# Turning the normalised rows by VectorE block transposes and a DRAM trip in a one-core language-model tower

## The reference

```
h  = weight[x] * keep_mask[x]                        # gather of rows, 32 x 512 x 256
n1 = layernorm(h)
u, res = split(n1 @ in_proj_w.T, [512, 256])
u  = causal depthwise conv of 4 taps along the tokens (u) + conv_b
delta = softplus(u @ dt_proj_w.T + dt_proj_b)        # 512 x 512
g  = u * sigmoid(delta)
y[t] = 0.9 * y[t-1] + 0.1 * g[t]                     # scan along the tokens
h  = h + y @ out_proj_w.T + res
n2 = layernorm(h)
xd = mx_quantise(n2)                                 # blocks of 32, fp6 grid, scaled back
h  = h + xd @ mx_quantise(ffn_weight).T + ffn_bias
```

## Time and profile before

| what | value |
|---|---|
| median of 3 runs | 1011.38 us (1007.56 to 1011.82) |
| profiled execution, its own time | 1011.74 us |
| its span from first to last instruction | 1009.9 us |
| PE busy | 970.3 us (96%) |
| PEld busy | 822.0 us (81%) |
| DVE busy | 854.6 us (85%) |
| ACT busy | 582.3 us (58%) |
| POOL busy | 743.1 us (74%) |
| chain that ended last | PE 93%, DVE 4%, POOL 1%, ACT 1%, DMA 1%, issue 1% |

### The profile page before, as it was taken

One profiled execution on the slowest core, in us unless ns is written; L12 is line 12 of the kernel. 1 busy time (PEld: TensorE's weight loads), 2 busy tenths in 40 slices (PEclk: granted clock), 3 DMA queues, 4 the chain that ended last, 5 costly groups with the idle time before them and its releaser, 6 DMA issues.

```text
span 1009.9 us, 15142 instructions
## 1 busy us (share of the span) xinstructions
PE 970.3 (96%) x5140; PEld 822.0 (81%) x5140; DVE 854.6 (85%) x1563; ACT 582.3 (58%) x966; POOL 743.1 (74%) x586
## 2 busy tenths in 40 slices
PE   3699999999999999999999999999999999999996
PEld 2477888888888888888888888888888888888885
DVE  4868988888988898888888898889888888889866
ACT  4455665565566565566556556656556655655441
POOL 5657777788777788777778877778877777886661
PEclk9799999999999999999999999999999999999997
DMA  4002122222211222211222221122221122221111
GB/s 152 22 21 63 55 56 80 83 64 85 76 55 56 83 62 83 83 55 54 78 83 62 83 77 55 55 83 62 83 83 53 56 78 83 63 84 64 42 43 42
DMA packets 51468, 68.28 MB, mean 68 GB/s; under 512 B 10096, under 2 KB 42736, under 8 KB 51440
## 3 DMA queue, kind: packets, MB, share of 16 engines
q1 hardware_dynamic: 45296, 51.08, 16.0%
q0 software_dynamic: 6144, 16.85, 6.4%
HBM read 35.40 MB, written 32.51 MB: 67 GB/s over the span
## 4 chain that ended last, share of the span: by engine, by line
PE 93%; DVE 4%; POOL 1%; ACT 1%; DMA 1%; issue 1%; DVEq 0%; POOLq 0%
PE psZ L991 12%; PE psZ L992 12%; PE psZ L998 12%; PE psT L949 6%; PE psT L945 6%; PE psT L946 6%; PE psU L934 6%; PE psU L930 6%; PE psU L931 6%; PE psO L1035 3%; PE psO L980 3%; PE psO L981 3%; PE psO L1036 3%; PE psO L982 3%; PE psO L1037 3%; PE psT L1049 3%
## 5 line engine op out<-in xcount | busy, mean ns | idle before, releaser
L356 POOL TENSOR_TENSOR g_lo<-g,g_hi 128x512 fp32r<-128x512 f32 x128 | 194.5, 1530 | 168.1 <-ACT g_hi L484 168.1
L683 DVE SCALAR_TENSOR_TENSOR u<-psU,cw,u 128x511 f32<-128x511 f32 x378 | 265.0, 743 | 18.6 <-ACT u L466 14.2
L991 PE MATMUL psZ<-u_hi,dt_hi 128*128 128x512 f32 x512 | 206.6, 404 | 10.3 <-ACT u_hi L473 7.1
L998 PE MATMUL psZ<-u_lo,dt_hi 128*128 128x512 f32 x512 | 204.1, 399 | 0.1
L992 PE MATMUL psZ<-u_hi,dt_lo 128*128 128x512 f32 x512 | 203.8, 398 | 0.0
L363 POOL TENSOR_TENSOR u_lo<-u,u_hi 128x512 fp32r<-128x512 f32 x128 | 163.3, 1299 | 15.3 <-ACT u_hi L473 14.0
L466 ACT ACTIVATE u<-psU,cb,cw 128x512 f32<-128x512 f32 x126 | 98.1, 779 | 121.8 <-PE psU L934 115.0
L477 ACT ACTIVATE psZ<-psZ,gate_b 128x512 f32<-128x512 f32 x128 | 84.5, 661 | 113.7 <-PE psZ L998 113.0
L341 POOL DMA_INDIRECT rows<-table,ids x128 | 126.3, 986 | 30.7 <-issue 29.4
L473 ACT ACTIVATE u_hi<-u 128x512 fp32r<-128x512 f32 x128 | 80.5, 629 | 91.9 <-DVE u L683 91.9
L767 DVE SCALAR_TENSOR_TENSOR g<-psZ,u 128x512 f32<-128x512 f32 x128 | 85.4, 687 | 45.6 <-ACT psZ L477 45.6
(11 more groups left out here) (107 smaller groups left out, 2186.7 us busy)
## 6 DMA issues: line engine op xcount, KB each, us to landing
out<-h SPq DMA_DIRECT2D x31, 512.0 KB, 2.9
turned<-xb SPq DMA_DIRECT2D x30, 512.0 KB, 2.8
xT<-turned SPq DMA_DIRECT2D x120, 128.0 KB, 3.5
rows<-table,ids POOLq DMA_INDIRECT x128, 2.9
dt_stage<-dt_wT SPq DMA_DIRECT2D x1, 1024.0 KB, 5.6
g<-in_wT SPq DMA_DIRECT2D x1, 768.0 KB, 4.6
ids<-x SPq DMA_DIRECT2D x32, 2.0 KB, 3.7
ow_stage<-out_wT SPq DMA_DIRECT2D x1, 512.0 KB, 7.4
```

What stands on the lines that cost most here:

```text
L356: pool.tensor_tensor(g_lo[:, m, :], g[:, m, :], f32(g_hi[:, m, :]), ALU.subtract).then_inc(g_lo_ready[m], 1)
L683: dve.scalar_tensor_tensor(u[:, m, back:T], u_psum_tile(st, m)[:, 0:T - back], cw[:, m, TAPS - 1 - back:TAPS - back], u[:, m, back:T], ALU ...
L991: pe.matmul(psZ[:, m % 2, :], dt_hi[:, k, o], u_hi[:, k, :], start=(k == 0), stop=False)
L998: ins = pe.matmul(psZ[:, m % 2, :], dt_hi[:, k, o], u_lo[:, k, :], start=False, stop=(k == M - 1))
```

## The change

The eight PE transposes of `n1` in each step go (the lead-in keeps its own), and `n1` is turned as `xd` is: `normalise1` writes it in the order of blocks, DVE transposes its 32x32 blocks into `nb_blocks` (`turn_n1`), SP writes those to `turned_n` in DRAM, waits, and reads them back in four DMAs into `nT` in SBUF. `nT_hi` and `nT_lo` are then made from `nT` on the same two engines as before. With this come changes of order: on DVE `turn_blocks` goes ahead of the convolution, gate 3 goes into the next step behind it, the taps of groups 0 and 1 alternate, `add_linear` goes ahead of `split_nT`, and gate 2 goes behind the quantisation; on ACT the first tap of group 1 goes ahead of `g_hi` 3, and `xT_hi` ahead of `u_hi` 3. The last step's `inverse_root2` on POOL is done in one part.

```diff
+        nb_blocks, nT = sb("nb_blocks", [P, C * D]), sb("nT", [P, C * D])
+        turned_n = nc.dram_tensor("turned_n", (P, C * D), F32, kind="Internal").ap()
...
+        n1_blocks = n1[:].rearrange("p c d -> p (c d)").rearrange("p (q k c j) -> p k q c j", q=Q, k=KD, c=C)
+        nT_by_token = nT[:].rearrange("p (a m i) -> p m a i", a=Q, i=BLOCK)
...
+                if st.front:
+                    sp.wait_ge(nT_lo_ready, s + 1)
+                    sp.wait_ge(n_turned, s + 1)
+                    sp.dma_start(turned_n, nb_blocks[:]).then_inc(n_written, 16)
+                    sp.wait_ge(n_written, 16 * (s + 1))
+                    for q in range(Q):
+                        blocks = turned_n.rearrange("(a j) (q n) -> q j a n", a=Q, q=Q)[q]
+                        sp.dma_start(nT[q * BLOCK:(q + 1) * BLOCK, :].rearrange("j (a n) -> j a n", a=Q),
+                                     blocks).then_inc(nT_loaded, 16)
...
-                    if later(s + 1):
-                        act.wait_ge(t1_psum, s + 1)
+                    if st.first:
+                        act.wait_ge(t1_psum, 1)
+                    elif st is not lead_in:
+                        act.wait_ge(n_turned, s)
...
 def split_nT():    # ACT
-                    act.wait_ge(t1_psum, s + 2)
+                    act.wait_ge(nT_loaded, Q * 16 * (s + 1))
...
-                    act.activation(nT_hi[:, nb], psT[:], ACT.Copy).then_inc(nT_hi_ready, 1)
+                    act.activation(by_token(nT_hi[:, nb]), nT_by_token, ACT.Copy).then_inc(nT_hi_ready, 1)
...
+                def turn_n1():
+                    dve.wait_ge(n1_ready, s + 2)
+                    if later(s):
+                        dve.wait_ge(n_written, 16 * s)
+                    dve.transpose(nb_blocks[:], flat(n1[:])).then_inc(n_turned, 1)
...
 def split_nT():    # DVE
+                    if st is not lead_in:
+                        dve.tensor_tensor(by_token(nT_lo[:, nb]), nT_by_token, f32(by_token(nT_hi[:, nb])),
+                                          ALU.subtract).then_inc(nT_lo_ready, 1)
+                        return
...
                 if st.tail:
                     dequantise(None, own=False)
-                convolve(0, 0, 1, 0, 1, 1)
-                if st.tail:
                     turn_blocks()
+                if st.back:
+                    gate(M - 1, s - 1)
+                convolve(0, 1, 0, 1, 0, 1)
+                if st.front:
+                    turn_n1()
...
+                if st.tail:
+                    add_linear(None)
                 if st.front:
                     split_nT()
-                if st.tail:
-                    add_linear(None)
                 if st.back:
                     block_max(None)
-                gate(2)
-                if st.back:
                     quantise()
                     dve.wait_ge(q_ready, s)
-                gate(3)
+                gate(2)
...
-                if st.front:
-                    transpose_n1()    # PE, between merge(1) and dt_proj_0_1((2, 3))
```

More of the change, by code:

```diff
@@ L192, in lm_tower_kernel @@
         turned_written, xT_loaded = sem("turned_written"), sem("xT_loaded")
+        n_turned, n_written, nT_loaded = (sem(n) for n in ("n_turned", "n_written", "nT_loaded"))
         xT_hi_ready, xT_lo_ready = sem("xT_hi_ready"), sem("xT_lo_ready")
@@ L376, in inverse_root2 @@
                     pool.wait_ge(var2_ready, s + (part or 0))
+                    if later(s - 1):
+                        pool.wait_ge(n2_ready, s - 1)
                     pool.tensor_tensor(rstd2[:, cs], ve2[:, cs], neg_half[:, cs],
@@ L390, in split_xT @@
                     pool.wait_ge(xT_hi_ready, s - 1)
-                    pool.tensor_tensor(by_token(xT_lo), xT_by_token, f32(by_token(xT_hi)),
+                    pool.tensor_tensor(by_token(xT_lo[:]), xT_by_token, f32(by_token(xT_hi[:])),
                                        ALU.subtract).then_inc(xT_lo_ready, 1)
@@ L425, in step @@
                 if st.back:
-                    for part in st.back_parts:
-                        inverse_root2(part)
+                    inverse_root2(None)
                 if st.main:
@@ L500, in normalise1 @@
                     act.wait_ge(nmr1_ready, s + 2)
-                    if later(s + 1):
-                        act.wait_ge(t1_psum, s + 1)
+                    if st.first:
+                        act.wait_ge(t1_psum, 1)
+                    elif st is not lead_in:
+                        act.wait_ge(n_turned, s)
                     for c in range(C):
-                        ins = act.activation(n1[:, c, :], h[:, ring, c, :], ACT.Identity, bias=nmr1[:, c:c + 1],
+                        to, h_c = n1[:, c, :], h[:, ring, c, :]
+                        if st is not lead_in:
+                            to, h_c = n1_blocks[:, :, :, c, :], h_c.rearrange("p (k q j) -> p k q j", k=KD, q=Q)
+                        ins = act.activation(to, h_c, ACT.Identity, bias=nmr1[:, c:c + 1],
                                              scale=rstd1[:, c:c + 1])
@@ L529, in split_xT @@
                         act.wait_ge(xT_loaded, Q * 16 * (s - 1))
-                        act.activation(by_token(xT_hi), xT_by_token, ACT.Copy).then_inc(xT_hi_ready, 1)
+                        act.activation(by_token(xT_hi[:]), xT_by_token, ACT.Copy).then_inc(xT_hi_ready, 1)
                         return
@@ L538, in split_nT @@
                 def split_nT():
-                    act.wait_ge(t1_psum, s + 2)
+                    if st is lead_in:
+                        act.wait_ge(t1_psum, 1)
+                        act.activation(nT_hi[:, nb], psT[:], ACT.Copy).then_inc(nT_hi_ready, 1)
+                        return
+                    act.wait_ge(nT_loaded, Q * 16 * (s + 1))
                     if later(s):
                         act.wait_ge(m_psum[1], s)
-                    act.activation(nT_hi[:, nb], psT[:], ACT.Copy).then_inc(nT_hi_ready, 1)
+                    act.activation(by_token(nT_hi[:, nb]), nT_by_token, ACT.Copy).then_inc(nT_hi_ready, 1)
                 if st is lead_in:
@@ L761, in add_linear, with gate @@
                                       ALU.add).then_inc(result_ready, 1)
-                def gate(m):
+                def gate(m, s=s):
                     dve.wait_ge(tanh_ready[m], s + 1)
@@ L837, in turn_blocks @@
                     dve.transpose(xb[:], flat(xd[:])).then_inc(xb_ready, 1)
+                def turn_n1():
[3 more added lines that the diff above has]
+                    dve.transpose(nb_blocks[:], flat(n1[:])).then_inc(n_turned, 1)
                 def split_nT():
                     dve.wait_ge(nT_hi_ready, s + 2)
-                    if later(s):
-                        dve.wait_ge(m_psum[1], s)
+                    if st is not lead_in:
+                        dve.tensor_tensor(by_token(nT_lo[:, nb]), nT_by_token, f32(by_token(nT_hi[:, nb])),
+                                          ALU.subtract).then_inc(nT_lo_ready, 1)
+                        return
                     dve.tensor_tensor(nT_lo[:, nb], psT[:], f32(nT_hi[:, nb]), ALU.subtract).then_inc(nT_lo_ready, 1)
@@ L1059, in transpose_n1 @@
                 def transpose_n1():
[L1060 to L1066, removed]
                     to_channels(lambda c, k: n1[:, c, k * P:(k + 1) * P], psT, t1_psum)
```

6 lines of the change are left out of this document (3 added, 3 removed).

## The result

The changed kernel takes 1021.62 us (median of 4 runs, 1019.36 to 1022.44), the kernel before, beside it, 1011.49. The ratio is 1.0106, with a 95% interval of 1.0076 to 1.0136: 10 us or 1% slower. The forecast was 1024 (994 to 1032), slower. The profiled execution's own time is 1021.15 us, its span 1019.3.

A forecast was written before the change was run, and what follows sets the result against it. PE bounds the kernel before at 29.83 us a step; afterwards a DVE, ACT and POOL loop of 30.30 us binds. 1011.74 + 13.6 - 0.9 = 1024.4, 0.36 less against the median: 1024 us, range 994 to 1032.

The forecast's parts named there:

- The layout: One middle step's DVE, ACT and POOL loop, counted from the variance instruction: 30.30 us against 29.83 before; chance 57%.
- POOL's stretch: POOL's run without a gap from g_lo 3 to the end of xT_lo, 15.96 us, ending at 30.36.
- this last term: Lead-in and steps 0, 1 and 31, without the loop: between 0 and -1.7 us, taken as -0.9.
- the wrong term: Trip of n1 through DRAM costs nothing; lead-in and first steps change by between 0 and -1.7 us each at most.
- The total of 1.3 us a step: PE's waiting in each middle step, about 1.3 us, most of it at linear for xT_lo.
- Two conflicts: DVE waits for POOL twice a step: nT_lo 0.97 us behind g_lo 0, the -mean instruction about 1.1 behind xT_lo.
- This mis-sized term: DVE reaches the small -mean instruction at 29.2 at the latest and waits about 1.1 us for xT_lo.
- Rival 2: nT_lo starts before g_lo 0, so POOL waits: loop 29.33 us, total 996.3 us; chance 15%.
- Its counterargument: With a shorter loop, add_linear and POOL's part both hang on the same xT_lo, restoring g_lo 0 first.
- Rival 3: DVE waits for POOL at nT_lo but not at the -mean instruction: loop 30.12 us, total 1019.2 us; chance 7%.
- Rival 1: Neither nT_lo nor the -mean instruction waits for POOL, PE stays the bound: 985.6 us; chance 9%.
- Rival 4: nT_lo waits for both g_lo, 1.27 us a step more, 1061; or late trip or lower PE clock; chance 9%.

The follow-up runs named there:

- e4: The changed kernel without the trip of n1 through DRAM, nT_hi and nT_lo reading nb_blocks directly; 1018.08 us.
- e6: The changed kernel with split_nT ahead of add_linear and the two small variance instructions moved from DVE to ACT; 985.02 us.
- e2: The changed kernel with nT_lo reading the PSUM tile psT in place of nT in SBUF, order unchanged; 995.6 us.
- e1: The changed kernel with split_nT put back ahead of add_linear on DVE, nothing else different; 996.66 us.
- e9: The changed kernel with DVE's old order around the gates, but split_nT still behind add_linear; 1013.9 us.
- e3: The changed kernel with DVE transposing only 32 of the 1024 columns of n1 (except in step 0); 1020.88 us.
- e5: The changed kernel with -mean and variance+eps of the second layernorm made on ACT in place of DVE; 1013.5 us.
- e7: The changed kernel with DVE's old order around the gates, split_nT ahead of add_linear; ACT's order as changed; 987.1 us.

## Why the prediction was right

**What bounds.** As forecast, PE's 0.87 us a step were given, and a loop of DVE, ACT and POOL took the bound over. The layout against the trace, counted from `ve` at 499.03:

| point | laid out | measured |
|---|---|---|
| gate 0 | 2.23 | 2.13 |
| `nT_lo` starts | 4.56 | 4.48 |
| `g_lo` 0 starts | 4.26 | 4.27 |
| block maxima start | 6.66 | 6.57 |
| gate 3 starts | 12.98 | 12.87 |
| POOL's stretch begins | 14.40 | 14.26 |
| `xT_lo` ends | 30.36 | 30.22 |
| next `ve` | 30.30 | 30.16 |

Every point held within 0.15 us. Against its own execution the forecast of 1024.4 was 3.3 us too high: 29 steps of 30.30 in place of 30.18 are 3.5 us too much. The rest is at the ends, where 29 x (30.18 - 29.83) = 10.1 us stand against a difference of the executions of 1021.15 - 1011.74 = 9.4: they gave back 0.7 us where 0.9 was taken.

That this last term came out is luck. The prediction had the trip through DRAM cost nothing and the first steps come out even or shorter. In the run the first `xT_lo` comes at 104.13 and in the kernel before at 102.42, 1.7 us late, and without the trip it would come at 100.96 (e4). The last steps gave back more than that, so the wrong term does not show in the sum.

**PE's waits.** The total of 1.3 us a step held (30.18 - 28.89, with e6's step for PE's list). That they would stand before `linear` held by half: in the step shown 0.64 us stand there and about 0.5 at L1033 and its neighbour, where PE waits for `u_lo` out of the same stretch of POOL.

**Two conflicts.** `nT_lo` waits 0.95 us (0.97 laid out). That it is the two SBUF inputs is shown by e2, and that it is the order by e1 and e9. L734 was laid out to wait about 1.1 us "at the latest" and waits 1.50, since DVE came to it 28.58 us after `ve` and not 29.2. This mis-sized term had no effect, as its end is set by `xT_lo`. The rule of the Trainium skill that the prediction weighed ("SBUF — State Buffer", section "SBUF: two separate sides"), on the port pair of VectorE and GpSimd, also fits e1, where the later one to start waits and it is then POOL. The word of the Trainium skill that the pair is held for the whole instruction fits less exactly: in e1 POOL's pair starts 0.27 us before `nT_lo` ends and becomes only 0.15 us longer.

**Hidden parts.** The trip was called free and is so in the middle, but not in the first two steps (e4). The transpose on DVE was reckoned into DVE's own 29.2 us ahead of its wait, and e3 shows that it costs nothing where it stands. The transpose of `xd` ahead of gate 3 is another matter: it lies on the loop. e3 did not touch it. POOL's stretch, called gapless, holds four short idle times before its gathers (0.15 to 0.31 us); they are in both kernels, and it is 15.96 us long in both (513.29 to 529.25 here), so the sum did not suffer.

**Rivals.** Rival 2 (`nT_lo` comes first) gave 996.3 by its working; e1, which makes it come first, took 996.66, with a mean step of 29.23 where 29.33 was laid out. Its counterargument, that `g_lo` 0 comes first again and again, held for the changed kernel: the mean of `nT_lo` over 31 instructions is 2105 ns (e2's table), which is 29 times about 2.17 and twice 1.22. Rival 3 (only `nT_lo` waits) gave 1019.2; the nearest run, e5, took 1013.5, as its step is 29.92 and not 30.12. Rival 1 gave 985.6; e6, without either wait, took 985.02. Rival 4 did not come.

**What the prediction did not see** is that the old order of the gates is better for the change than its new one (e7 against e1): there gate 3 comes early enough for its `g_lo` although POOL is twice disturbed.

## What to carry to other kernels

Moving work off the bounding engine pays only until the next loop through the other engines binds. Lay that loop out from the last wait to itself, with the instructions' durations as they are beside their new neighbours. When a VectorE instruction changes from a PSUM input to a second SBUF input, look at what GpSimd runs at that moment, and place it so that VectorE starts first and GpSimd, if it has slack, waits. Work that is hidden in the middle steps can still cost in the first ones (e4). A high busy share may be waiting: compare an instruction's duration with its usual one before calling an engine full.

## What the runs showed of the hardware

- A DVE instruction of 128x1024 with two SBUF inputs takes 1.21 to 1.22 us alone and 1.95 to 2.19 us behind a GpSimd `tensor_tensor` of 128x512 that started 0.19 to 0.43 us before it (e5; 2.14 to 2.19 in the changed kernel). With one input in PSUM it takes 1.22 us in the same place (e2).
- It got in between two GpSimd instructions issued back to back, in each of 29 steps of the changed kernel; GpSimd's second one then waited (3.52 us for the pair in place of 2.54).
- A 128x4 `tensor_scalar` in SBUF waits for GpSimd's current instruction as well (1.67 us in place of 0.17), while DVE's transposes of 32x32 blocks, 128x1024, keep 1.23 to 1.25 us, one of them at 510.73 beside a `g_lo` that ran from 510.21 to 511.75. That `g_lo` is 0.24 us longer than usual; it began before DVE's dequantisation, with two SBUF inputs, had ended at 510.60, and no run parts the two.
- A second 512 KB written to DRAM and read back by 32-partition blocks every step cost the middle steps 0.03 us each (DMA share 0.36 with 104 GB/s, against 0.24 with 69 GB/s in e4). In the first step, rows gathered beside it came 1.63 us later.
